# Group norms of a four-layer network: where x is loaded, who builds the tap diagonals, who normalizes

## The reference

```
x = x + L0(gn(x))      # two depthwise 3x3 convolutions, an SSD scan, an MLP
x = x + L1(gn(x))      # in-projection, depthwise 3x3 + SiLU, a 4-direction selective scan, out-projection
x = x + L2(gn(x))      # one depthwise 3x3 convolution and a bias
x = x + L3(gn(x))      # the same with other weights

def _gn(v, G=32, eps=1e-5):         # per sample: 32 groups of 6 channels over all pixels
    m = mean(v over a group); s = var(v over a group)
    return (v - m) / sqrt(s + eps)
```

## Time and profile before

| | us |
|---|---|
| median of three runs | 28435.44 (28420.39 to 28436.43) |
| the profiled execution | 28430.92 |
| its span | 28429.4 |
| VectorE's wait for x, 16 waits | 180.9 |
| TensorE busy | 25357.2 (89%) |
| VectorE busy | 23856.0 (84%) |
| GpSimd busy | 22128.3 (78%) |
| ScalarE busy | 20735.5 (73%) |

### The profile page before, as it was taken

One profiled execution on the slowest core, in us unless ns is written; L12 is line 12 of the kernel. 1 busy time (PEld: TensorE's weight loads), 2 busy tenths in 40 slices (PEclk: granted clock), 3 DMA queues, 4 the chain that ended last, 5 costly groups with the idle time before them and its releaser, 6 DMA issues. The chain is left out here.

```text
span 28429.4 us, 291694 instructions
## 1 busy us (share of the span) xinstructions
PE 25357.2 (89%) x80480; PEld 11869.3 (42%) x80480; DVE 23856.0 (84%) x23376; ACT 20735.5 (73%) x38376; POOL 22128.3 (78%) x9798
## 2 busy tenths in 40 slices
PE   8899888998889988899888998889988899888998
PEld 3444334443344433444334443344433444334443
DVE  6799867998679986799867998679986799867998
ACT  4788647886478864788647886478864788647886
POOL 3799737997379973799737997379973799737997
PEclk8999989999899998999989999899998999989999
DMA  0111101111011110111101111011110111101111
GB/s 8 51 63 64 45 8 51 63 64 45 8 51 63 63 46 8 51 63 63 46 8 51 63 63 46 8 51 63 64 45 8 51 63 64 45 8 51 63 64 45
DMA packets 833671, 1309.75 MB, mean 46 GB/s; under 512 B 224897, under 2 KB 242177, under 8 KB 828929
## 3 DMA queue, kind: packets, MB, share of 16 engines
q1 hardware_dynamic: 832000, 1290.45, 14.6%
HBM read 1223.00 MB, written 67.11 MB: 45 GB/s over the span
## 5 line engine op out<-in xcount | busy, mean ns | idle before, releaser
L1592 PE MATMUL ps<-arena,ident 128*128 128x512 f32 x24576 | 11670.0, 601 | 50.9 <-DVE arena L1419 50.8
L1407 DVE TENSOR_TENSOR_SCAN arena<-ps,arena 128x512 f32<-128x512 f32 x6144 | 7492.6, 1261 | 329.5 <-issue 208.0
L1407 DVE TENSOR_TENSOR_SCAN arena<-arena,ps 128x512 f32<-128x512 f32 x6144 | 7413.5, 1257 | 121.7 <-ACT arena L1786 101.9
L1960 POOL TENSOR_TENSOR arena<-arena 128x1536 f32<-128x1536 f32 x2048 | 7067.8, 3457 | 146.2 <-DVE arena L1407 144.6
L1592 PEld LDWEIGHTS ps<-arena,ident 128*128 128x128 f32 x24576 | 4349.8, 192 | 4544.5 <-issue 4240.7
L1970 POOL TENSOR_TENSOR arena<-arena 128x1536 f32<-128x1536 f32 x1728 | 5971.4, 3463 | 52.8 <-ACT arena L1806 52.8
L1797 ACT ACTIVATE scaled<-arena,cols 128x384 f32<-128x384 f32 x8192 | 4711.4, 605 | 1032.5 <-PE ps L1560 1025.5
L1786 ACT ACTIVATE ps<-arena 128x512 f32<-128x512 f32 x6144 | 4123.6, 684 | 602.2 <-DVE arena L1407 592.6
L1786 ACT ACTIVATE arena<-arena 128x512 f32<-128x512 f32 x6144 | 4251.2, 716 | 100.1 <-PE ps L1592 99.0
L1560 PE MATMUL ps<-ident,scaled 128*128 128x128 f32 x24576 | 3612.6, 277 | 590.3 <-DVE arena L1407 420.1
L1560 PEld LDWEIGHTS ps<-ident,scaled 128*128 128x128 f32 x24576 | 2854.6, 141 | 3050.1 <-DVE arena L1407 1583.7
(11 more groups left out here) (187 smaller groups left out, 32595.1 us busy)
## 6 DMA issues: line engine op xcount, KB each, us to landing
arena<-rows SPq DMA_DIRECT2D x3776, 256.0 KB, 3.2
spare<-rows SPq DMA_DIRECT2D x576, 256.0 KB, 3.4
arena<-x SPq DMA_DIRECT2D x16, 1536.0 KB, 13.0
x<-arena SPq DMA_DIRECT2D x16, 1536.0 KB, 10.7
arena<-x SPq DMA_DIRECT2D x64, 384.0 KB, 8.7
out<-arena SPq DMA_DIRECT2D x64, 384.0 KB, 3.0
rows<-xd SPq DMA_DIRECT2D x256, 64.0 KB, 2.7
arena<-L_conv_fc_w SPq DMA_DIRECT2D x16, 576.0 KB, 5.2
```

The lines of the kernel that those rows point to most:

```text
L1407: nc.vector.tensor_tensor_scan(flip(states(b, n, t)), flip(decays), flip(adds), carry[:, k, N2 * n + t:N2 * n + t + 1], ALU.mult, ALU.add) ...
L1592: nc.tensor.matmul(m.ps[:, t, :], m.ident[:, :], states(b, n, t), start=False, stop=(n == SUMS[t][-1])).then_inc(at[Y_MM[t]], 1)
L1960: nc.gpsimd.tensor_tensor(three(dbu[:, no % DB, :]), du[:, b % 2, :, :], each, ALU.mult).then_inc(at["db_ready"], 1)
```

## The change

1. x of the first sample is loaded before the loop, in a stage of its own, with one DMA into slots 6 and 7 (xin). In the loop, the last convolution's SyncE list begins with the two DMAs that bring the next sample's x into xin; the wait for them comes behind the output DMAs. The array x has a ninth sample, a copy of the first, so that the last turn has something to load. Norm A reads xin, and ScalarE copies it to s01 (two instructions of 4096 columns), where the rest of layer 0 expects it.
2. The tap diagonals of the four group norms are made by ScalarE (activation Copy with the weight as scale), at the end of its list of the stage; GpSimd has nothing to do in these stages. The taps built in the SSD stage stay on GpSimd.
3. VectorE normalizes the first half and a quarter of the second; the other three quarters of the second half (3072 columns) are one ScalarE activation with scale 1/sigma and bias -mean/sigma. The bias is one new small VectorE instruction behind the reciprocal.

```diff
--- before.py
+++ after.py
@@ -161,7 +161,7 @@
     return m.nc.vector.bn_stats(m.gn_stats[:, half, bass.ds(i * 6, 6)], x)
 
 
-def group_norm(m, src, dst, taps, load=None, loads=(), have_stats=False):
+def group_norm(m, src, dst, taps, loads=(), have_stats=False, keep=None):
 
 
 
@@ -170,21 +170,15 @@
     m.start(10)
     mv = m.take(NH, 2, parts=P)
     dev = m.take(NH, parts=P)
-    names = ("loaded_0", "loaded_1", "stats_done", "mean_mm", "var_in", "var_mm", "chain", "rstd_in", "rstd_out",
-             "brought") + Taps.NAMES
-    with Stage(nc, *names) as (*loaded, stats_done, mean_mm, var_in, var_mm, chain, rstd_in, rstd_out, brought,
+    shift = m.take(NH, parts=P)
+    cut = L // 4
+    names = ("stats_done", "mean_mm", "var_in", "var_mm", "chain", "rstd_in", "rstd_out", "shift_done", "brought") + Taps.NAMES
+    with Stage(nc, *names) as (stats_done, mean_mm, var_in, var_mm, chain, rstd_in, rstd_out, shift_done, brought,
                                taps_loaded, centre), nc.Block() as block:
         @block.sync
         def _(sp):
-            for h in range(NH):
-                if load is not None:
-                    sp.dma_start(src[:, h, :], load[:, h, :]).then_inc(loaded[h], 16)
             taps.sync(sp, taps_loaded)
             bring(m, sp, brought, loads)
-
-        @block.gpsimd
-        def _(pool):
-            taps.gpsimd(pool, taps_loaded, centre)
 
         @block.vector
         def _(dve):
@@ -197,8 +191,6 @@
                 dve.wait_ge(chain, n)
 
             for h in range(NH):
-                if load is not None:
-                    dve.wait_ge(loaded[h], 16)
                 if not have_stats:
                     for i in range(NT):
                         ins = block_stats(m, src[:, h, i * T:(i + 1) * T], h, i)
@@ -214,14 +206,21 @@
             nc.vector.tensor_scalar(m.gn_rstd[:, :], m.ps[0:P, 1, 0:NH], 1e-5, None, ALU.add).then_inc(rstd_in, 1)
             dve.wait_ge(rstd_out, 1)
             link(nc.vector.reciprocal(m.gn_rstd[:, :], m.gn_rstd[:, :]))
-            for h in range(NH):
-                nc.vector.tensor_scalar(dst[:, h, :], src[:, h, :], m.gn_mean[:, h:h + 1], m.gn_rstd[:, h:h + 1],
+            nc.vector.scalar_tensor_tensor(shift, m.gn_mean[:, :], -1.0, m.gn_rstd[:, :], ALU.mult, ALU.mult).then_inc(shift_done, 1)
+            for h, end in ((0, L), (1, cut)):
+                nc.vector.tensor_scalar(dst[:, h, 0:end], src[:, h, 0:end], m.gn_mean[:, h:h + 1], m.gn_rstd[:, h:h + 1],
                                         ALU.subtract, ALU.mult)
 
         @block.scalar
         def _(act):
+            if keep is not None:
+                for h in range(NH):
+                    nc.scalar.copy(keep[:, h, :], src[:, h, :])
             act.wait_ge(rstd_in, 1)
             nc.scalar.activation(m.gn_rstd[:, :], m.gn_rstd[:, :], ACT.Sqrt).then_inc(rstd_out, 1)
+            act.wait_ge(shift_done, 1)
+            nc.scalar.activation(dst[:, 1, cut:], src[:, 1, cut:], ACT.Identity, scale=m.gn_rstd[:, 1:2], bias=shift[:, 1:2])
+            taps.scalar(act, taps_loaded, centre)
 
         @block.tensor
         def _(pe):
@@ -249,6 +248,18 @@
         sp.dma_start(self.w, self.weight.rearrange("(t p) k -> p t k", p=self.parts)).then_inc(loaded, 16)
         with nc.allow_non_contiguous_dma(reason="a few words a partition"):
             sp.dma_start(self.b, columns(self.bias, self.parts)).then_inc(loaded, 16)
+
+    def scalar(self, act, loaded, centre):
+
+        nc, w = self.m.nc, self.w
+        act.wait_ge(loaded, 32)
+        if self.own:
+            nc.scalar.activation(w[:, :, 4:5], w[:, :, 4:5], ACT.Identity, bias=1.0).then_inc(centre, 1)
+            act.wait_ge(centre, 1)
+        for t in range(self.n):
+            for i, tap in enumerate(PE_TAPS):
+                nc.scalar.activation(self.diag[:, t * len(PE_TAPS) + i, :], self.m.ident[0:self.parts, 0:self.parts], ACT.Copy,
+                                     scale=w[:, t, tap:tap + 1])
 
     def gpsimd(self, pool, loaded, centre):
 
@@ -305,12 +316,16 @@
             taps_mm, taken, tapped, side_done, filled, gathered, side_added, silu_out, stored, brought), nc.Block() as block:
         @block.sync
         def _(sp):
-            bring(m, sp, brought, loads)
             if out is not None:
+                for to, of in loads:
+                    sp.dma_start(to, of).then_inc(brought, 16)
                 for i, (t, r) in enumerate(steps):
                     sp.wait_ge(side_added, i + 1)
                     sp.dma_start(rows(out, t, r), rows(dst, t, r)).then_inc(stored, 16)
+                sp.wait_ge(brought, 16 * len(loads))
                 sp.wait_ge(stored, 16 * len(steps))
+            else:
+                bring(m, sp, brought, loads)
 
         @block.gpsimd
         def _(pool):
@@ -2271,14 +2286,20 @@
         Stage.held = None
         constants(m)
         x1v = x1.rearrange("(t p) l -> p t l", p=P)
+        xin = m.slots(6, NH, P)
+        with Stage(nc, "first_in") as (first_in,), nc.Block() as block:
+            @block.sync
+            def _(sp):
+                sp.dma_start(xin, x[0].rearrange("(t p) l -> p t l", p=P)).then_inc(first_in, 16)
+                sp.wait_ge(first_in, 16)
         with nc.Fori(0, samples) as b:
-            xb = x[bass.ds(b, 1)].rearrange("a (t p) l -> p (a t) l", p=P)
+            x_next = x[bass.ds(b + 1, 1)].rearrange("a (t p) l -> p (a t) l", p=P)
             ob = out[bass.ds(b, 1)].rearrange("a (t p) l -> p (a t) l", p=P)
             s01, s23, s45 = m.slots(0, NH, P), m.slots(2, NH, P), m.slots(4, NH, P)
 
 
             taps = Taps(m, NH, P, l0["cpe1_w"], l0["cpe1_b"], own=True, side=10)
-            group_norm(m, s01, s23, taps, load=xb)
+            group_norm(m, xin, s23, taps, keep=s01)
             taps_2 = Taps(m, NH, P, l0["cpe2_w"], l0["cpe2_b"], own=True, side=10)
             weights, loads = ssd_weights(m, l0)
             conv3x3(m, s23, s45, taps, loads=loads, **TWO)
@@ -2304,7 +2325,7 @@
             conv3x3(m, s23, s45, taps, residual=s01, **ONE)
             taps = Taps(m, NH, P, l3["w"], l3["b"], side=10)
             group_norm(m, s45, s23, taps)
-            conv3x3(m, s23, s01, taps, residual=s45, out=ob, **ONE)
+            conv3x3(m, s23, s01, taps, residual=s45, out=ob, loads=[(xin[:, h, :], x_next[:, h, :]) for h in range(NH)], **ONE)
             nc.all_engine_barrier()
 
 
@@ -2325,6 +2346,7 @@
     v = np.asarray(v)
     if name == "x":
         v = v.transpose(0, 3, 1, 2).reshape(v.shape[0], C, L)
+        v = np.concatenate([v, v[:1]])
     elif name in ("in_proj_w", "out_proj_w", "fc1_w", "fc2_w"):
         v = v.T
     elif name in ("cpe1_w", "cpe2_w", "conv_w"):
```

## The result

The changed kernel takes 28305.58 us, the median of six runs (28300.25 to 28311.61); the kernel before took 28424.08 us beside it (28419.79 to 28436.43). The ratio is 0.9957, 95% interval 0.9946 to 0.9969: 118.5 us or 0.42% faster. The profiled executions have spans of 28307.8 and 28429.4 us, 121.6 apart.

What follows compares the result with a forecast made beforehand. No engine is full; between barriers of all engines only the last to arrive counts. Load -78, first sample +6 and norms -36 make -108 us from 28435.4: 28327, stated as 28326, range 28285 to 28380.

Steps and rivals of the forecast that it cites:

- The load: Start of samples 1 to 7: x loaded ahead saves 11.2 us before the normalization, seven times, 78 us.
- the half microsecond named as a sign: Turns to samples 1 to 7: if right, statistics begin within 0.5 us of the engines' return.
- The first sample: Before the loop: statistics wait for the whole load and a barrier, a loss of 5.8 us, once.
- Norms: Group norms A (layer 0) to D (layer 3), normalization's start (t0) to next stage: 5.90, 6.91, 5.56, 5.56 us; -36 us.
- C and D: Norms of layers 2 and 3: ScalarE's part and eight diagonals, 5.25 us, plus 0.31 to the next stage, 5.56.
- A's excess: Layer 0's norm: adding 1 to the centre tap and waiting for it, +0.34 us, making 5.90.
- The price of a diagonal: ScalarE's tap diagonals in the norms: 0.27 us for 96 columns, 0.29 for 128, from start to start.
- The sentence on the alternative: All normalization on VectorE, diagonals on ScalarE ahead of its start: all four norms 5.02 us, -67 us instead of -36.
- rival (d): TensorE's clock, at 0.50 throughout the norms: shorter norms shift its rise, 20 us either way; inside the forecast's 0.84.
- (a): Top of the loop: the load's gain is absent, only the norms' remains; 28405 us, no measurable change; chance 0.05.
- (b): Table loads after Sqrt: new 1.28 us loads cost 32 norms 41 to 82 us, 28367 to 28408; chance 0.04.
- (c): ScalarE's 288 diagonals slower: at 0.50 us each 64 us more, 28390; at 0.80, 28476; chance 0.03.

Runs made afterwards that it cites:

- e1: Changed kernel with only x loaded ahead and the keeping copies; diagonals on GpSimd, normalization on VectorE as before; 28363.9 us against 28428.6.
- e2: Kernel before with only the tap diagonals moved to ScalarE, behind Sqrt; 28341.0 us against 28428.6.
- e6: e5 with ScalarE's normalization part cut to 512 columns in layer 1's norm and 1,536 in layer 2's; 28256.8 us against 28427.3.
- e3: Kernel before with only the normalization split between VectorE and ScalarE (3,072 columns); diagonals on GpSimd; 28334.5 us against 28428.6.
- e4: Changed kernel without the split: the whole normalization on VectorE, diagonals on ScalarE behind Sqrt, x loaded ahead; 28304.1 us against 28428.6.
- e5: Changed kernel with ScalarE's diagonals ahead of Sqrt in the norms of layers 0 and 3; 28279.4 us against 28427.3.
- e9: e6 plus unread TensorE products: nine beside the statistics of layers 0 and 3, four behind every norm's variance; 28183.7 us against 28427.3.
- e12: e9 with three added products instead of four behind the variance in the norms of layers 1 and 2; 28193.8 us against 28428.1.
- e11: Changed kernel plus unread TensorE products: nine beside the statistics of layers 0 and 3, three behind every norm's variance; 28319.0 us against 28426.8.

## Why the prediction was right

The forecast of 28326 was 20 us above the measured 28305.58. Some 11 of them lie in the median of before, which is 28424.08 over six runs and not the 28435.44 of the first three; the other 10 are in the difference, -118.5 for -108.

1. **The load.** 11.2 us a turn were predicted, 24.57 - 13.50 = 11.07 measured, 77.5 in all for 78. VectorE's return, which could not be seen before, is 0.29 us behind ScalarE's in the mean, for the 0.15 assumed; at two turns (0.68 and 0.56) it is just beyond the half microsecond named as a sign. The outputs were not held up: they are issued and land as before. e1 shows the gain by itself.
2. **The first sample.** +5.8 predicted, 34.38 - 28.56 = +5.82.
3. **Norms.** Predicted 5.90, 6.91, 5.56, 5.56; measured 5.78, 6.94, 5.53, 5.53; -36 for -37.8. (The terms written down for C and D add to 5.28 before the last 0.31, not to 5.25, which is without weight; A's excess was the centre tap, 0.22 us for the 0.34 assumed.) The price of a diagonal (0.27 and 0.29 us from start to start) was right: eight in 2.21 us, twelve in 3.60, and that was because the row of the same operation was taken and not GpSimd's. ScalarE was last in all four. The sentence on the alternative, -67 us with the normalization whole on VectorE, is e2's sum to the microsecond, though e2 has the diagonals beside the normalization and not ahead of it.
4. **The rest.** -12 us that the sum does not have: 4.4 behind C, 4.2 in the last convolution (behind D less the turns' 77.5), 5.7 behind A, less 2.1 behind B. The first two go with the clock at the convolutions' start: in sample 0 it is 0.88 for 0.79 in the fifth to eighth microsecond of C's, 0.98 for 0.88 in D's. Between two levels of 0.50 and 1.00 that is a rise some 0.7 us sooner in C, and that convolution takes 70.41 us for 70.75. It doesn't follow from shorter norms: D's norm became longer (5.53 for 5.01), and e6 with the shortest norm C (4.28) has 0.79 and 70.8 again. What moves the rise is open. Behind A is the SSD stage's scatter. All this was rival (d), put in the range at +-20. It held the change, in part by luck: e3 and e4 differ by 92 us behind A alone, 46 either way, where I had allowed 20, and with e4's sum behind A the changed kernel would have come out 38 us slower, near 28343. The range, 38 us either way before it was widened, is also less than the sum of its own terms, 50 us. (d) itself misread the clock, which is not at 0.50 throughout the norms. In norm C of the kernel before it was at 1.00 at first and fell about the time of t0 (3408.60):

```profile
3404.50:3406.40 1.90, 0.00 (x0) 0.00 (x0) 1.53 (x4) 1.00 (x1) 0.00 (x0) 1.00 0.01 1
3409.60:3411.00 1.40, 0.00 (x0) 0.00 (x0) 1.40 (x2) 0.00 (x0) 1.40 (x1) 0.50 0.00 0
```

5. **The rivals.** (a) fell with e1. (b) fell: of the table loads, 24 stand before Sqrt and 8 more before the copies of norm A, none behind Sqrt; I had counted one load there and it is two, both covered. (c) fell with the diagonals' price.

```profile
L220 ACT ACT_TABLE_LOAD x24 | 30.8, 1283 | 165.5 <-PEq L644 121.1 <-PEq L2223 44.3
L218 ACT ACT_TABLE_LOAD x8 | 10.3, 1283 | 99.1 <-issue 78.0 <-PEq L2290 21.1
```

The prediction priced the diagonals alone, but not the split alone, and so did not say that parts 2 and 3 work against each other: alone they are worth 67 and 51 us in the norms, together 38. The Trainium skill (ScalarE: Activation LUTs, section Rules for kernel authors) says that multiplies and adds belong on VectorE. The trace agrees where ScalarE took 3,072 columns and had the diagonals behind them (B and C at 6.94 and 5.53 us, 5.03 and 5.01 in e4). It does not where ScalarE's part was cut to 512 and 1,536 columns (e6, 4.84 and 4.28), nor in A and D once the diagonals were made earlier (e5, 3.49 instead of 5.02).

## What to carry to other kernels

At a barrier only the last engine counts, so give each engine its work by the time at which it is free and not by its speed: diagonals in ScalarE's idle time before the statistics end, and a share of the normalization sized by what ScalarE has left to do, made 61 us of norms out of the same instructions. Judge edits of a microsecond by the stretch that they touch, summed over all its repeats, since a clock that rises elsewhere can move the total by as much as the edit. And added products on an idle TensorE paid here in full only where the granted clock was up when they ended and still up when the real work started, so look at the clock's rows there and not only at when the products end; they cost up to 3 us a norm where they themselves became the last to end.

## What was not expected of the hardware

- GpSimd stands still while VectorE normalizes: one 0.52 us instruction took 4.63 us beside both halves (4.76 us), 2.63 beside one (2.40), 1.01 beside a quarter (0.80), and 0.53 with no VectorE work.
- The stretch behind norm A takes 760, 769 or 777 us in samples of one execution of e1 (757 to 780 over all runs), and the longest have TensorE at 1.2 GHz through 20 us in which the shortest have it mostly at 2.4.
- In e9 to e12 the convolution behind norm C took 67.64 us where it began at 2.4 GHz and 70.1 to 70.95 where TensorE's added products ended at 1.2 GHz, although three of these slow ones (e12) had products up to 0.63 to 0.84 us before it and one fast one (e11) none for 1.34 us.
